# Image 0 convolved alone first, w1 and w2 turned late, gate comparison in small steps, and one tap of v on ScalarE and GpSimd for pairs 0 to 3

## The reference, cut to what matters

```
x = x + L0(gn(x));  x = x + L1(gn(x))          # gn: group norm, 32 groups of 3 channels
L0: qkv = einsum(w_qkv, x); qkv = 3x3 depthwise conv(qkv)
    q, k normalised over the 256 pixels; scores = q k^T * temperature (8 heads of 12 channels)
    out = softmax(scores) v; out = w_proj out
L1: scores = softmax(x_flat @ gate_w + gate_b); the two best of 4 experts, ranks 0 and 1
    top_w = softmax(top_v); present[rank] = experts that any pixel chose with that rank
    coef = present^T top_w                      # a weight for each expert and pixel
    y_e = w2[e] relu(w1[e] x + b1[e]) + b2[e]; out = sum_e coef_e y_e
```

## Time and profile before

| what | value |
|---|---|
| median of three runs | 169.04 us (168.91 to 170.16) |
| profiled execution | 170.19 us, its span 168.4 us |
| busy share of the span | PE 88%, DVE 86%, PEld 70%, ACT 60%, POOL 27% |
| chain that ended last | PE 44%, DVE 42%, issue 7% |
| granted PE clock, mean | 0.990 |

### The profile page before, as it was taken

The page is one execution under the profiler, slowest core; times in us unless marked ns, Lnnn a source line. Parts: engine busy times, 40 slices in busy tenths (PEclk is TensorE's granted clock), DMA queues, the critical chain, the costliest instruction groups (busy, mean ns, idle before and its releaser), DMA issues.

```text
span 168.4 us, 3554 instructions
## 1 busy us (share of the span) xinstructions
PE 148.9 (88%) x1275; PEld 118.6 (70%) x1275; DVE 144.0 (86%) x389; ACT 101.4 (60%) x227; POOL 45.4 (27%) x63
## 2 busy tenths in 40 slices
PE   0486896999998999999999899898999798999963
PEld 0476795999998999999999899675674242333322
DVE  2579999877999999999799699659779999999992
ACT  3075087565928639379399147485499768675710
POOL 5130220540514235425246225451227000000000
PEclk9999999699999999999999999999999999999999
DMA  6994305041140410503204100000000000112313
GB/s 151 226 232 103 70 0 157 6 134 26 38 124 0 133 29 0 155 9 85 76 2 117 44 0 6 0 0 2 4 0 0 0 0 0 47 47 58 90 47 93
DMA packets 8810, 9.72 MB, mean 58 GB/s; under 512 B 3640, under 2 KB 7512, under 8 KB 8792
## 3 DMA queue, kind: packets, MB, share of 16 engines
q1 hardware_dynamic: 8648, 9.25, 21.8%
q10 hardware_dynamic: 144, 0.24, 0.4%
HBM read 2.94 MB, written 1.57 MB: 27 GB/s over the span
## 4 chain that ended last, share of the span: by engine, by line
PE 44%; DVE 42%; issue 7%; DMA 2%; ACT 2%; POOL 1%; DVEq 0%; POOLq 0%
DVE v_acc L1136 9%; PE qk_ps L720 8%; PE qk_ps L722 8%; DVE h_mixed L1395 5%; PE out_ps L809 4%; DVE stats L1092 3%; PE sc_ps L774 3%; PE sc_ps L784 3%; PE qk_ps L725 3%; DMA x_sb<-in_x 2%; PE v_ps L766 2%; DVE wc L1021 2%; DVE x_sb L1403 2%; PE small_ps L826 2%; PE v_ps L969 2%
## 5 line engine op out<-in xcount | busy, mean ns | idle before, releaser
L1136 DVE SCALAR_TENSOR_TENSOR v_acc<-v_ps,v_taps,v_acc 96x576 f32<-96x576 f32 x64 | 51.8, 809 | 1.2
L720 PE MATMUL qk_ps<-w_a,x_a 128*128 128x192 f16 x243 | 46.6, 245 | 0.0
L722 PE MATMUL qk_ps<-w_b,x_b 128*128 128x192 f16 x243 | 46.5, 245 | 0.0
L720 PEld LDWEIGHTS qk_ps<-w_a,x_a 128*128 128x128 f16 x243 | 24.6, 101 | 0.2
L722 PEld LDWEIGHTS qk_ps<-w_b,x_b 128*128 128x128 f16 x243 | 23.6, 97 | 0.3
L527 ACT ACTIVATE h_mixed<-qk_ps,slope 128x512 f32<-128x512 f32 x24 | 16.9, 775 | 5.4 <-PE qk_ps L946 5.3
L725 PE MATMUL qk_ps<-w_c,x_c 96*128 96x192 f16 x81 | 20.1, 248 | 0.0
L479 ACT ACTIVATE sc_exp<-sc_qk,neg_max 96x12 f32<-96x12 f32 x16 | 4.7, 296 | 21.3 <-DVE neg_max L1175 21.3
L640 POOL TENSOR_TENSOR sq_sum<-qk_sq 128x384 f32<-128x384 f32 x8 | 8.0, 1002 | 32.8 <-ACT qk_sq L441 25.1
L1395 DVE TENSOR_TENSOR h_mixed<-h_mixed,hidden 128x512 f32<-128x512 f32 x24 | 15.0, 679 | 0.0
L1092 DVE BATCH_NORM_STATS2 stats<-x_sb 96x6 f32<-96x256 f32 x32 | 11.7, 412 | 3.0 <-DMA x_sb<-in_x 2.8
(11 more groups left out here) (200 smaller groups left out, 349.9 us busy)
## 6 DMA issues: line engine op xcount, KB each, us to landing
x_b<-x_a SPq DMA_DIRECT2D x7, 324.0 KB, 3.1
x_sb<-in_x SPq DMA_DIRECT2D x8, 192.0 KB, 4.8
out<-xs SPq DMA_DIRECT2D x7, 192.0 KB, 2.1
x_a<-x_lo SPq DMA_DIRECT2D x7, 108.0 KB, 2.7
x_b<-x_lo SPq DMA_DIRECT2D x7, 108.0 KB, 2.5
x_c<-x_lo SPq DMA_DIRECT2D x21, 36.0 KB, 1.9
wdw_all<-in_L_conv_w_dw SPq DMA_DIRECT2D x1, 648.0 KB, 6.3
w_sb<-in_L_conv_w SPq DMA_DIRECT2D x2, 144.0 KB
```

Source lines behind the costliest of these rows:

```text
L720: eng.matmul(to, window(x_a[p][:, dx, b], half, dy), w_a[:, t, :], start=(t == 0), stop=False, skip_group_check=True)
L722: mm = eng.matmul(to, window(x_b[p][:, dx, b], half, dy), w_b[:, t, :], start=False, stop=False, skip_group_check=True)
L1136: eng.scalar_tensor_tensor(out=v_acc[i % 3][:, :, :], in0=v_window(dy, dx), scalar=v_taps[:, t:t + 1], in1=v_acc[i % 3][:, :, :], op0=ALU. ...
```

## The change

**Start.** The scaled taps (`dw_scaled`) are multiplied with w_qkv before the turn: `combine(0, 3)` and `combine(3, 6)` on DVE, taps 6 to 8 on ACT (`last_taps`). PE turns 18 blocks (`turn_taps`) into five PSUM banks, and `high_weights` and `low_weights` take two taps at a time from there. `wdw_all` and its DMA are gone. ACT normalises pair 0 one image after the other; DVE shifts image 0 (`shift_image`), and PE convolves image 0 (tiles 0 and 1, plain) while image 1 is still prepared. Tiles 2 and 3 of pair 0 are now packed: SP waits for five weight banks, sends the five weight DMAs, then `pack(0)` (six DMAs), and only then loads pairs 3 to 7.

**Loop.** In pairs 0 to 3 (`ONE_TAP`) the tap (1, 1) is made by ACT into `v_one` right behind the centre tap, and POOL adds it to `v_acc` once DVE's seven are done (`add_tap`). `copy_qk` stands before `centre_tap`. Chain 3 covers one pair and chain 4 the two x pairs 6 and 7 and the first two of the second block. w_proj is turned in pair 1, w1 in pair 5 (with `prep_w1` on DVE at the end of pair 4, `low_w1` at the end of pair 5), w2 in pair 6. Gates 0 and 1 stand after tile 3, gate 2 after the loop.

**Hidden tiles and gates.** Comparison is six operations on parts of 16 to 48 columns, without the ties; hidden tiles 2 and 6 go to ACT; the orders of PE, ACT, DVE and POOL are altered. **Tail.** ACT makes the b2 part (`bias_tile`) and POOL adds it to `x_sb`; DVE's `add` is a plain sum; `last_second` goes tile by tile over both halves in two other banks.

The diff, cut to its core, and indented less:

```diff
-CHAIN_COLS = [(0, 2), (2, 6), (6, 10), (10, 16), (16, 20), (20, 24), (24, 26), (26, 30), (30, 32)]
+CHAIN_COLS = [(0, 2), (2, 6), (6, 10), (10, 12), (12, 20), (20, 24), (24, 26), (26, 30), (30, 32)]
...
-X_CHAIN = [0, 1, 1, 2, 2, 3, 3, 3]
+X_CHAIN = [0, 1, 1, 2, 2, 3, 4, 4]
...
-STATS_BEFORE = [1, 3, 5, 9, 10, 12, 13, 15, 16]
-RELU_DVE = (2, 6, 18, 20, 22)
+STATS_BEFORE = [1, 3, 5, 7, 10, 12, 13, 15, 16]
+RELU_DVE = (18, 20, 22)
+ONE_TAP = (0, 1, 2, 3)
...
-w0_ps = hid_ps[0:2]
+w0_ps = [out_ps[:, :], hid_ps[0]]
 y_ps = [mix_ps[:, :], v_bank[0]]
+y_last = [v_bank[1], hid_ps[1]]
+wc_ps = [qk_ps[0], sc_ps, out_ps, mix_ps, qk_ps[1]]
...
-    eng.dma_start(x_a[p][C:128], x_lo[p][0:32]).then_inc(packed[p], 16)
-    eng.dma_start(x_b[p][C:128], x_lo[p][32:64]).then_inc(packed[p], 16)
+    eng.dma_start(x_a[p][C:128, :, b], x_lo[p][0:32, :, b]).then_inc(packed[p], 16)
+    eng.dma_start(x_b[p][C:128, :, b], x_lo[p][32:64, :, b]).then_inc(packed[p], 16)
     for dx in range(3):
-        eng.dma_start(x_c[p][32 * dx:32 * dx + 32], x_lo[p][64:C, dx]).then_inc(packed[p], 16)
+        eng.dma_start(x_c[p][32 * dx:32 * dx + 32, b], x_lo[p][64:C, dx, b]).then_inc(packed[p], 16)
 load(0)
 eng.dma_start(wqkv_sb[:, :, :], w_qkv.rearrange("(s o) c -> o s c", s=3)).then_inc(in_w, 16)
 eng.dma_start(wdw_sb[:, :, :], w_dw.rearrange("(s o) a b c -> o s (a b c)", s=3)).then_inc(in_w, 16)
-eng.dma_start(wdw_all[:, :], w_dw[0:QK].rearrange("o a b c -> (o a b c)").unsqueeze(0)
-              .broadcast_to([C, QK * TAPS])).then_inc(in_dw, 16)
 load(1)
...
-for i in range(3, PAIRS):
-    load(i)
...
+eng.wait_ge(wc_hi_set, 5)
...
+pack(0)
+for i in range(3, PAIRS):
+    load(i)
...
+def last_taps(first, last):
+    eng.wait_ge(dw_set, 1)
+    for t in range(first, last):
+        for s in range(2):
+            a = eng.activation(wc[:, t, s * C:(s + 1) * C], wqkv_sb[:, s, :], ACT.Copy,
+                               scale=dw_scaled[:, t, s:s + 1])
...
+def other_tap(i):
+    n = ones_before(i)
+    wait(eng, v_done, n - 1)
+    eng.activation(v_one[n % 2][:, :, :], v_window(1, 1), ACT.Copy, scale=v_taps[:, 8:9]).then_inc(v_one_set, 1)
...
+def normalise_first():
+    eng.wait_ge(norm_done, 1)
+    eng.wait_ge(pads_set, 1)
+    for b in range(2):
+        eng.activation(xs[0][:, b * HW:(b + 1) * HW], x_sb[:, 0, b * HW:(b + 1) * HW], ACT.Identity,
+                       scale=rstd[:, b:b + 1], bias=shift[:, b:b + 1]).then_inc(xs_ready, 1)
+        eng.wait_ge(xs_ready, b + 1)
+        src = xs[0][:, b * HW:(b + 1) * HW].rearrange("c (h w) -> c h w", w=W)
...
+def bias_tile(i):
+    wait(eng, x1_biased, i - 1)
+    eng.activation(b2_part[i % 2][:, :], w0_ps[i % 2][0:C, :], ACT.Identity, scale=bias_col[:, 0:1],
+                   bias=bias_col[:, 1:2]).then_inc(b2_ready, 1)
...
+copy_constants()
 square_dev(0)
-normalise(0)
-high_weights(0)
-eng.copy(wv_hi[:, :], out_ps[0:C, 0:C]).then_inc(wv_set, 1)
-shift_high(0)
-high_weights(1)
-high_weights(2)
+last_taps(6, TAPS)
+normalise_first()
+eng.wait_ge(wvT_ready, 1)
+eng.copy(wv_hi[:, :], small_ps[0:C, 96:96 + C]).then_inc(wv_set, 1)
+for g in range(5):
+    high_weights(g)
+shift_high_second()
 for i in range(PAIRS):
+    if i > 0:
+        copy_qk(i - 1, 1)
...
+        other_tap(i)
     if i > 0:
-        take_qk(i - 1, 1)
+        square_qk(i - 1, 1)
     if i == 0:
         square_dev(TURN_CHAIN[i])
     if i + 1 < PAIRS:
...
+    if i == 1:
+        copy_proj()
+    if i == 5:
+        copy_w1()
+    if i == 6:
+        copy_w2()
...
+relu(2)
 heads_exp(7)
 relu(3)
 take_mix(7)
+gate_exps(0)
+square_dev(7)
 relu(4)
-square_dev(7)
-gate_exps(0)
 relu(5)
+relu(6)
 square_dev(8)
 normalise2(5)
+high_xn2(5)
+normalise2(6)
 relu(7)
-normalise2(6)
 normalise2(7)
+high_xn2(6)
 relu(8)
-high_xn2(5)
 relu(9)
+high_xn2(7)
+top_exps(0)
 relu(10)
-high_xn2(6)
-relu(11)
-high_xn2(7)
-relu(12)
-top_exps(0)
-relu(13)
 gate_exps(1)
-for h in (14, 15, 16):
+for h in range(11, 16):
     relu(h)
 take_u(0)
-for h in (17, 19, 21):
+for h in (16, 17, 19, 21):
     relu(h)
 coefs(0)
-top_exps(1)
 relu(23)
 eng.wait_ge(bias_done, 1)
 eng.copy(bias_col[:, :], small_ps[0:C, BIAS:BIAS + 2]).then_inc(bias_ready, 1)
+eng.wait_ge(bias_ready, 1)
 coefs(1)
-coefs(2)
-take_u(1)
-for i in range(3, PAIRS):
+bias_tile(0)
+bias_tile(1)
+top_exps(1)
+for i in range(2, PAIRS):
+    if i == 4:
+        take_u(1)
     coefs(i)
+    bias_tile(i)
...
+def low_first():
+    for b in range(2):
+        eng.wait_ge(hi_mid, b + 1)
+        eng.tensor_tensor(inner(x_lo[0], 1)[:, b], xs[0][:, b * HW:(b + 1) * HW].rearrange("c (h w) -> c h w", w=W),
+                          inner(x_a[0], 1)[:, b], ALU.subtract).then_inc(lo_mid, 1)
...
+def add_tap(i):
+    n = ones_before(i)
+    eng.wait_ge(v_one_set, n + 1)
+    eng.wait_ge(tap_done, taps_before(i + 1))
+    eng.tensor_tensor(v_acc[i % 3][:, :, :], v_acc[i % 3][:, :, :], v_one[n % 2][:, :, :], ALU.add)\
+       .then_inc(v_done, 1)
...
+    if i - 1 in ONE_TAP:
+        add_tap(i - 1)
...
+for i in range(PAIRS):
+    eng.wait_ge(b2_ready, i + 1)
+    eng.tensor_tensor(x_sb[:, i, :], x_sb[:, i, :], b2_part[i % 2][:, :], ALU.add).then_inc(x1_biased, 1)
...
+def prepare_v():
+    eng.wait_ge(wv_scaled_set, 1)
+    eng.wait_ge(norm_done, 1)
+    eng.wait_ge(in_c, 16)
...
+def turn_taps(first, last):
+    for t in range(first, last):
+        for s in range(2):
+            at = tap_columns(t).start + s * C
+            mm = eng.transpose(wc_ps[t // 2][0:C, at:at + C], wc[:, t, s * C:(s + 1) * C],
...
-    if i == 0 or i == 1 and n == 0:
+    if i == 0 and n < 2 or i == 1 and n == 0:
...
             hi, lo = (window(x[p][0:C, dx, b], half, dy) for x in (x_a, x_lo))
             eng.matmul(to, hi, w_a[0:C, t, :], start=(t == 0), stop=False, skip_group_check=True)
             eng.matmul(to, hi, w_b[0:C, t, :], start=False, stop=False, skip_group_check=True)
             mm = eng.matmul(to, lo, w_a[0:C, t, :], start=False, stop=(t == TAPS - 1),
                             skip_group_check=True)
     else:
-        if first == 0 and i == 1 and n == 1:
...
-keep_warm(3)
-prepare_qkv()
-keep_warm(6)
-project_v(0)
+keep_warm(2)
+eng.wait_ge(wc_set, 1)
+turn_taps(0, 3)
+prepare_v()
+eng.wait_ge(wc_set, 2)
+turn_taps(3, 6)
+eng.wait_ge(wc_last, 3)
+turn_taps(6, TAPS)
...
     conv_taps(i, 0, 0, TAPS)
+    if i == 0:
+        project_v(0, (1,))
...
+    if i == 1:
+        prepare_proj()
+    if i == 5:
+        prepare_w1()
+    if i == 6:
+        prepare_w2()
     conv_taps(i, 3, 0, 3)
-    if i >= 5:
-        gate(i - 5, {5: 5, 6: 6, 7: 7}[i], 0)
     if i >= 1:
...
-    if i == 0:
-        prepare_late()
+    if i in (5, 6):
+        gate(i - 5, {5: 5, 6: 6}[i], 0)
     if i + 1 < PAIRS:
         project_v(i + 1)
 first(0)
 gram(7)
+gate(2, 7, 0, 24)
 first(1)
...
+mix_heads(7)
 first(4)
-mix_heads(7)
-first(5)
 norm_means(7, 3)
 apply_mix(7)
...
 turn_u(0)
 first(20)
...
     mm = eng.matmul(small_ps[0:EXPERTS, 16 + r:17 + r], present_bf[:, r, :], ones_bf[:, 0:1],
                     start=True, stop=True)
 mm.then_inc(count_done, 1)
-first(21)
-first(22)
...
+    elif i == 1:
+        wait_hidden_taken(eng, HT - 4)
     else:
         eng.wait_ge(coef_set, MT * (i - 1))
-        eng.wait_ge(x1_biased, i - 1)
+        eng.wait_ge(b2_ready, i - 1)
     c = i // 4
...
 weight(0)
-first(23)
-weight(1)
+first(21)
+first(22)
 eng.wait_ge(cols_step, 2)
 eng.matmul(small_ps[0:C, BIAS:BIAS + 2], b2_sb[:, :], slope_cols[:, :], start=True, stop=True)\
    .then_inc(bias_done, 1)
+first(23)
+weight(1)
...
     for m in range(MT):
+        if i == 2 and m == 2:
+            turn_u(1)
...
-keep_warm(3, mix_ps[:, 256:512])
+        wait_hidden_taken(eng, HT - 1 - 2 * b)
+    for m in range(MT):
+        eng.wait_ge(mixed_done, MT * i + m + 1)
+        for b in range(2):
+            t = slice(b * HW, (b + 1) * HW)
+            mm = eng.matmul(y_last[b][0:C, t], w2T[:, m, :], h_mixed[i % 2][:, m, t], start=(m == 0),
+                            stop=(m == MT - 1))
+            if m == MT - 1:
+                mm.then_inc(y_done, 1)
...
+def scale_taps():
     eng.wait_ge(prep, 4)
-    eng.tensor_tensor(wqkv_scaled[:, :, :], wqkv_sb[:, :, :],
...
+def combine(first, last):
+    n = last - first
+    eng.wait_ge(dw_set, 1)
+    eng.tensor_tensor(wc[:, first:last, :].rearrange("p t (s c) -> p t s c", s=2),
+                      wqkv_sb[:, 0:2, :].unsqueeze(1).broadcast_to([C, n, 2, C]),
+                      dw_scaled[:, first:last, :].unsqueeze(3).broadcast_to([C, n, 2, C]), ALU.mult)\
...
+            eng.wait_ge(v_one_set, ones_before(i) + 1)
+    for n in range(lo, min(hi, taps_of(i))):
         dy, dx = OUTER[n]
         t = 3 * (dy + 1) + dx + 1
...
-    eng.tensor_tensor(ties[:, t, :].rearrange("p t (e j) -> p t e j", e=EXPERTS), score_j, score_e,
-                      ALU.is_equal).then_inc(compared, 1)
+    if c == 0:
+        eng.wait_ge(beaten_zero, 1)
+    for e in range(EXPERTS):
```

(63 more changed lines are left out.)

302 lines of the change are left out of this document (167 added, 135 removed).

## The result

The changed kernel takes 180.72 us (median of four runs, 178.46 to 181.52) against 169.08 in the same session: slower, ratio 1.0596 (95% interval 1.0502 to 1.069). The ratio leaves out the runs at 181.19 and 181.52 as disturbed and goes by the two at 178.46 and 180.24. Its profiled execution took 178.46 us, span 176.3, against 170.19 and 168.4 before. The forecast was 166.0, range 163.0 to 168.9: wrong in sign.

What follows compares the result with a forecast made beforehand. It took DVE's taps to bound pair 0, PE pair 2, step order the middle, PE and DVE the tail. Loop -4.8, middle +1.7, tail -0.65, POOL +0.7 gave -3.05: 166.0 us, range 163.0 to 168.9.

Steps and rivals of the forecast that it cites:

- Start: Start and pair 0: image 0 convolved earlier, `project_v(1)` at 26.3 instead of 27.53, -1.2 us; nearest bounds -2.8 and -0.7.
- the forecast wait: Pair 0: PE done with tile 1 at 18.5 waits 2.6 us for `pack(0)`, then a clock fall costing 1.65.
- Pairs 1, 3, 6, 7: Loop terms: pair 1 -1.55, pair 3 -1.05 (waits for means and v), pair 6 -0.3, pair 7 -1.6 us.
- -1.55: Pair 1: the fall of PE's clock is gone if it came already in pair 0, half of 3.3 less 0.1.
- Pair 4: Fourth pair of taps: they start late, behind statistics and eight means, but end with PE; no cost charged.
- Pair 5: Pair 5 at 12.1 instead of 11.2 us, with `prep_w1` and `low_w1` between taps and six more PE transposes: +0.9.
- Hidden tiles: Loop's end to first `coefs`: gate 2 +0.9, ACT's wait +1.6, `take_u(0)` +0.9, last stretch -1.7; together +1.7, bounds 0 and +2.7.
- Small comparison: Gates: six small operations, 0.6 us against 1.71 a chunk, free DVE by 1.1 twice, but off the path.
- Tail: Steady tail: PE stays at 3.08 us a pair, DVE goes from 3.12 to 2.5; -0.65 us, before POOL's +0.7.
- POOL's part: POOL's work beside DVE's two-input SBUF operations: one held operation charged, in `gate_scores(1)`, +0.7 us, bounds 0 and +2.4.
- the cover of 0.03 us: Steady tail: DVE's period of 3.05 us beside POOL's add stays under PE's 3.08, so POOL's add costs nothing there.
- the third rival: Tail: POOL's add becomes DVE's bound, 3.8 us a pair, 5.1 on top; 171.1 us, chance 0.09.

Runs made afterwards that it cites:

- a1: The changed kernel with seven more warm-up matmuls before the first conv (six instead of two, and three more behind the turned taps): 181.36 us, ratio 1.0716.
- a3: The changed kernel with POOL's eight additions of the b2 part left out, so the output lacks b2: 174.59 us, ratio 1.0312.
- b2: b1 with DVE adding the b2 part instead of POOL, and the scores, weights and split of chunk 1 moved earlier: 166.16 us, ratio 0.9805.
- a4: The changed kernel with no pair giving its last tap to ACT and POOL (`ONE_TAP` empty): 177.73 us, ratio 1.0491.
- b4: The kernel before with only the comparison changed to six operations on 16 to 48 columns: 167.62 us, ratio 0.9893.
- b3: b2 with the warm-up matmuls of a1, plus five before the variances of chain 1 and four before tile 2 of pair 0: 165.64 us, ratio 0.9784.
- b1: a2 with `prep_w1` moved on DVE from the end of pair 4 into its wait in pair 0: 170.9 us, ratio 1.0077.
- a2: The changed kernel with `take_logits(5, 3)` and `gate_logits(1)` ahead of `gate_weights(0)` and `gate_split(0)` on DVE: 172.69 us, ratio 1.0188.
- c3: b3 with `take_u(0)` behind `relu(16)` and `bias_tile(0)` ahead of `coefs(1)` on ACT: 164.67 us, ratio 0.9715.

## Why the prediction was wrong

*Start (-1.2, measured 0).* The conv's start was right (12.1, measured 12.49), and so was the pack (21.1, measured some 21.4). The step that failed is the one on warm-ups: with a low clock at the first conv matmul tile 0 would end `some 2 us later`, and the wait for `pack(0)` would cover it. The pace of the lower level did not end with tile 0; it lasted to 24.7, so PE came to tile 2 1.9 us after the pack, and made some nine matmuls of it at 0.16 (0.7 us). That took the place of the forecast wait and of the fall behind it (1.65): 0.3 + 1.9 + 0.7 - 1.65 is 1.25, the 1.2 that was lost. (PE was not `nearly idle from 8.5 to 11.5` either: the transposes stand there, 8.49 to 11.85.) When warm-ups make PE fast, a wait for the pack does come (a1: 0.91 us), and a fall that costs 1.9, but behind the wait for DVE ahead of it.

*A wait's length alone does not decide the fall.* I took the fall of one execution as the price of a wait of 1.6 us. In the traces kept here PE waits 1.43 to 1.80 us 19 times between 14 and 160 us, three times right behind warm-up matmuls, and its clock falls within 3 us behind five of these waits (the kernel before's 1.59, two in a1, one each in a3 and b2). Behind the wait of 2.37 us it falls in all four traces that have it (the changed kernel, a1, a3, a4).

*Pairs 1, 3, 6, 7.* Right in sign, -3.75 measured for -4.5. But pair 1's part is no gain of the change. The fall of clock whose end I counted as -1.55 is in the profiled execution of the kernel before, and not in b4's, whose pair 1 is 0.7 us shorter than the changed kernel's. In the experiments' sessions executions of the kernel before at a granted clock of 0.999 or more took 168.48 to 169.06 us (one 172.03), those below it 169.80 to 171.52. So the median of 169.04 most likely has no such fall, and -1.55 should not have been laid on it. *Pair 4* (+0.63) was put at nothing; no run took it apart, and it stays in b3 (11.51 us). PE waits 0.20 us there for the means of chain 4 and 0.22 for the last tap; the cause of the rest is open.

*Pair 5 (+0.9, measured +2.03).* The step was mis-sized. I said that PE had 1 us in hand there, and took 1.65 us from `prep_w1`'s first to its last step as the price; it took 2.2, and the lateness moved `k_diag` beside a POOL operation, so that PE waited 1.45 us for it. b1 gives 1.68 back by placing the same eight operations in a 3.9 us wait of DVE in pair 0.

*Hidden tiles (+1.7, measured +5.89).* The mechanism was forecast, with ACT's wait at 2.0 (2.36) and `take_u(0)` at 0.9 (0.93). What failed is the sentence that costs PE's wait at its own length. The fall of clock behind such a wait stands in the earlier trace rows, and I charged it in pair 0 and not here, where it was 2.7 us. Most of the rest: PE's waits there are 2.67 us (0.30 and 2.37) where I had 2.0, and the 0.4 of old waits that I took off did not go (0.58 and 0.23 us now, 0.61 and 0.21 before). a2 removes wait and fall, 5.1 of span.

*Small comparison.* I found it off the path in the changed kernel, and counted the end of PE's wait for `present_bf` in the -1.7. That -1.7 came (4.26 us before, 2.65 now). In the kernel before the small comparison is on the path: b4 gains 1.4 us by it alone.

*Tail (+0.05, measured +3.15).* The order's part was right: -0.65, and a3 against the kernel before gives -0.7. POOL's part was +0.7 and came as 3.8, by two steps. For `gate_scores(1)` I took one held operation; `g_prob`, `top_all` and, behind them, the cast to `u_tok` were held, 2.2 us of DVE and 1.9 of the tail, within the bound of 2.4. For the steady tail `for half of that DVE is in add, which reads PSUM` is the step that failed. POOL's addition takes 1557 ns on average, up to 2.80, not 1.25, as each side delays the other, and the last four begin and end inside `mix`. So DVE's period became 3.5, not 3.05, and the cover of 0.03 us was gone, as the third rival said. Its price of 5.1 for that part was too high: 1.95 was measured. That it lies near the 4.0 us of span that a3 gives for both parts is luck. The Trainium skill (SBUF — State Buffer, Who interferes with whom) states that two SBUF inputs on DVE contend with GpSimd's reads; a3 agrees (883 to 691 ns), and I had charged one operation and left the 24 of `mix` to the cover.

*What stays open.* The profiled execution (178.46 us) has a granted clock of 0.981; the other that the ratio goes by took 180.24 at 0.933, and no trace of it was kept. More of the same falls are likely, as a1's profiled execution has one in pair 6 (0.89), but they aren't shown for the changed kernel. That also leaves open most of the distance between the medians (11.64 us) and the spans (7.9). In b1 the profiled execution is 1 us below the median, and 2.3 us of its start are pace, of which pair 1 gives back 0.8: PE was fast from 15.7 us on, where a2 was slow to 24.8. That was not controlled; what b1 shows by itself is pair 5.

## What to carry to other kernels

Price a wait of PE not at its length alone: look for what its clock did behind waits of that length, in several executions, and charge that at every new wait by how often it came. One profiled execution can hold a fall that the median has not. Before moving a two-input SBUF operation to POOL, count all DVE operations with two SBUF inputs that it can stand beside, for the period of a balanced stage has no room for them. In a program whose engines run hand-written orders, look for the engine that waits for a step standing behind others it doesn't need: three reorderings without any operation less (a2, b1, c3) gave 5.1 (of span), 1.8 and 1.0 us.

## What the runs showed that was not expected

Up to 24.7 us the changed kernel's conv matmuls of 192 columns are 0.16 us apart (the pace of 1.2 GHz), while the profile's clock for the same stretch says 1.00 (line 12.49:27.49 above). In a1 the same spacing goes with 0.50 (23.40:26.00), behind a stretch at full pace. a3 has both in one execution: 0.16 us at 1.00 from 13.1 to 18.1, then 0.16 us at 0.50 from 22 to 24. So in these traces the clock column says nothing of a low clock that was there from the start, and the spacing must be read until the column first changes.

When the pace rises at the start differs between executions of kernels whose first 15 us are alike: 15.7 us in b1, 24.8 in a2.

POOL's addition and DVE's multiplication delay each other: the one 1.56 us on average and up to 2.80, the other 883 ns against 684.
